# First layer of a graph network on one core: W0's lower half applied to x's rows in the preparation

## What is computed

```python
# first part: W is (512, 256)
support = segment_sum(edge_weight[:, None] * x[dst], src, N)
out = relu(concat([x, support], axis=1) @ W + b)
x = layernorm(x + out)
# second part: twice
#   xl = x @ Wl; xr = x @ Wr
#   attention of 8 heads over the edges and each node's own loop; x = x + gelu(tmp)
x = layernorm(x + second_part(x))
```

## Time and profile before

| | us |
|---|---|
| median of 3 runs | 2466.81 (2465.28 to 2472.84) |
| the profiled execution | 2466.77 |
| its span, first to last instruction | 2464.9 |
| busy in the span: TensorE / DVE / ACT / POOL | 1895.9 / 1766.4 / 1339.7 / 1449.3 |
| mean granted clock of TensorE | 0.916 of 2.4 GHz |

### The profile page before, as it was taken

The page is one execution under the profiler, slowest core; times in us unless marked ns, Lnnn a source line. Parts: engine busy times, 40 slices in busy tenths (PEclk is TensorE's granted clock), DMA queues, the critical chain, the costliest instruction groups (busy, mean ns, idle before and its releaser), DMA issues. The chain is left out here.

```text
span 2464.9 us, 38027 instructions
## 1 busy us (share of the span) xinstructions
PE 1895.9 (77%) x8650; PEld 1357.2 (55%) x8650; DVE 1766.4 (72%) x4022; ACT 1339.7 (54%) x5172; POOL 1449.3 (59%) x1606
## 2 busy tenths in 40 slices
PE   0655656556489998779999999986779999999975
PEld 0434434444267775456666666653456666666654
DVE  8544333333256666669999999988579999999976
ACT  0255555555300003438788777853458777787833
POOL 3277777787700001577777677735677777777712
PEclk9777788888789999989999999998899999999988
DMA  3287575665478871255555555541255555555542
GB/s 99 73 193 172 172 172 171 167 171 170 114 246 267 269 261 46 79 148 158 157 152 160 153 147 153 151 104 35 73 156 159 155 151 156 151 152 151 143 98 96
DMA packets 225173, 369.91 MB, mean 150 GB/s; under 512 B 40436, under 2 KB 168438, under 8 KB 224983
## 3 DMA queue, kind: packets, MB, share of 16 engines
q1 hardware_dynamic: 160311, 195.75, 28.6%
q0 software_dynamic: 64512, 171.82, 24.9%
q10 hardware_dynamic: 160, 0.20, 0.0%
HBM read 272.59 MB, written 101.50 MB: 152 GB/s over the span
## 5 line engine op out<-in xcount | busy, mean ns | idle before, releaser
L1150 POOL DMA_INDIRECT gath<-gather_table,SRCI x880 | 835.1, 949 | 323.4 <-issue 262.9
L1371 ACT ACTIVATE gath<-gath 128x32 f32<-128x32 f32 x3264 | 710.8, 306 | 0.0
L1202 PE MATMUL p_sums<-gath,OH 128*128 128x272 f32 x1760 | 474.4, 410 | 101.7 <-DVE gath L1097 60.8
L723 POOL DMA_INDIRECT rows_by_src<-gath,node x440 | 433.5, 985 | 137.5 <-issue 116.9
L657 PE MATMUL p_expd<-X,HOTS 128*128 x880 | 290.6, 490 | 230.2 <-DVE HOTS L616 218.6
L1202 PEld LDWEIGHTS p_sums<-gath,OH 128*128 128x128 f32 x1760 | 319.3, 194 | 215.7 <-issue 141.5
L657 PEld LDWEIGHTS p_expd<-X,HOTS 128*128 128x128 f32 x880 | 205.5, 244 | 304.7 <-issue 269.9
L1172 PE MATMUL p_expd<-node,LBC 128*128 x2640 | 327.5, 274 | 0.0
L1172 PEld LDWEIGHTS p_expd<-node,LBC 128*128 128x128 bf16 x2640 | 260.3, 99 | 59.4 <-issue 1.7
L1244 DVE TENSOR_REDUCE scores<-work 128x32 f32<-128x1056 f32 x220 | 274.6, 1248 | 5.7
L1166 PE MATMUL p_expd<-gath,ident 128*128 128x512 f32 x440 | 236.9, 620 | 39.7 <-DMA gath<-gather_table,SRCI 39.7
(11 more groups left out here) (291 smaller groups left out, 2749.3 us busy)
## 6 DMA issues: line engine op xcount, KB each, us to landing
gath<-rows_by_src SPq DMA_DIRECT2D x122, 514.0 KB
LBC<-hots_by_node SPq DMA_DIRECT2D x220, 128.0 KB
HOTS<-hots_by_edge SPq DMA_DIRECT2D x220, 128.0 KB, 2.4
LBC<-local_rows SPq DMA_DIRECT2D x110, 128.0 KB, 3.5
hots_by_node<-gath SPq DMA_DIRECT2D x110, 128.0 KB, 4.5
hots_by_edge<-gath SPq DMA_DIRECT2D x110, 128.0 KB, 3.1
gath<-gather_table,SRCI POOLq DMA_INDIRECT x880, 2.8
rows_by_src<-gath,node POOLq DMA_INDIRECT x440, 4.2
```

The lines of the kernel that those rows point to most:

```text
L723: pool.indirect_dma_start(sup_d[:, :], bass.IndirectOffsetOnAxis(POSI[:, i:i + 1], 0), U[:, q % 4, g, :], None, bounds_check=EP - 1, oob_i ...
L1150: pool.indirect_dma_start(ROWS[:, i % (RING * G), 0:XW], None, tab_d[:, :], bass.IndirectOffsetOnAxis(SRCI[:, i:i + 1], 0)).then_inc(gathe ...
L1202: ins = pe.matmul(sums[k][:, 0:RW], OH[:, a % 2, g, :], slots(a, g, g + 1)[:, 0, :], start=(g % 2 == 0), stop=(g % 2 == 1))
L1371: ins = act.activation(R[:, h * C:(h + 1) * C], R[:, h * C:(h + 1) * C], ACT.Copy, scale=R[:, D + h:D + h + 1])
```

## The change

- In the preparation, x is loaded from ACT's queue near the start, and W0's lower half into W0B. TensorE turns each tile of x and multiplies it by W0's lower half, 22 tiles ahead of the products at L472 and 3 behind the sum at L478; ACT copies both (`flat`, `kept`) into TURNED.
- The scatter stage takes rows of TURNED in place of x, and its sums with the upper half and the bias go into SUP.
- The sum stage adds on top of that; POOL's clearing goes.
- The linear stage has no transposes and products of "h". hidden() is one instruction a tile, with the statistics of a group together. The remainder moves from DVE to POOL.

```diff
-        FIRST_PART = gath[:, 4 * G * UW:4 * G * UW + NT * D].rearrange("p (t d) -> p t d", d=D)
+        TURNED = node[:, 9984:9984 + NT * D].rearrange("p (t d) -> p t d", d=D)
...
@@ preparation, SP's queue
-                    sp.dma_start(Xv[:, 0:NT - 1, :], x[0:(NT - 1) * P, :].rearrange("(t p) d -> p t d", p=P)).then_inc(x_loaded, 16)
-                    sp.dma_start(Xv[0:TAIL, NT - 1, :], x[(NT - 1) * P:N, :]).then_inc(x_loaded, 16)
...
@@ preparation, ACT
                     load_edges(act, SIi, src, src_in)
+                    act.dma_start(W0B.rearrange("p (k n) -> p k n", k=2), W0[2 * P:4 * P, :].rearrange("(k p) n -> p k n", p=P)).then_inc(w0_in, 16)
+                    act.wait_ge(pad_set, 4)
+                    act.dma_start(Xv[:, 0:NT - 1, :], x[0:(NT - 1) * P, :].rearrange("(t p) d -> p t d", p=P)).then_inc(x_loaded, 16)
+                    act.dma_start(Xv[0:TAIL, NT - 1, :], x[(NT - 1) * P:N, :]).then_inc(x_loaded, 16)
+
+                    def flat(t):
+                        act.wait_ge(x_turned, t + 1)
+                        if t >= 2:
+                            act.wait_ge(x_prod, t - 1)
+                        act.activation(XTP[:, t % 2, :], psum_tr[t % 2][:, 0:D], ACT.Copy).then_inc(x_flat, 1)
+
+                    flat(0)
+                    for t in range(NT):
+                        if t + 1 < NT:
+                            flat(t + 1)
+                        act.wait_ge(x_prod, t + 1)
+                        act.activation(TURNED[:, t, :], psum_tr[2 + t % 2][:, 0:D], ACT.Copy).then_inc(x_kept, 1)
...
@@ preparation, TensorE
+                    def by_weights(first, last):
+                        for t in range(first, last):
+                            if t + 1 < NT:
+                                turn(t + 1)
+                            pe.wait_ge(x_flat, t + 1)
+                            if t >= 2:
+                                pe.wait_ge(x_kept, t - 1)
+                            for k in range(2):
+                                ins = pe.matmul(psum_tr[2 + t % 2][:, 0:D], XTP[:, t % 2, k * P:(k + 1) * P], W0B[:, k * D:(k + 1) * D],
+                                                start=(k == 0), stop=(k == 1))
+                            ins.then_inc(x_prod, 1)
...
+                    pe.wait_ge(consts, 12)
+                    pe.wait_ge(x_loaded, 32)
+                    pe.wait_ge(w0_in, 16)
+                    turn(0)
+                    by_weights(0, PART_B)
                     pe.wait_ge(consts, 13)
                     pe.wait_ge(ranks_ready, 1)
...
                     ins.then_inc(pos_summed, 1)
+                    by_weights(PART_B, NT)
+                    pe.wait_ge(x_kept, NT)
                     pe.wait_ge(rows_ready, 1)
...
@@ scatter stage, DVE and TensorE
-                            dve.tensor_tensor(FIRST_PART[:, t, :], turn[t % 2][:, 0:D], VEC[:, 0, :], ALU.add).then_inc(x_added, 1)
+                            dve.tensor_tensor(SUP[:, t, :], turn[t % 2][:, 0:D], VEC[:, 0, :], ALU.add).then_inc(x_added, 1)
...
-                                            Xv[:, bass.ds(tiles[g // 2], 1), :], start=True, stop=True)
+                                            TURNED[:, bass.ds(tiles[g // 2], 1), :], start=True, stop=True)
...
@@ sum stage, POOL
-                    pool.memset(SUP, 0.0).then_inc(cleared, 1)
...
@@ linear stage, POOL
+                        remainder(pool, t, LR[:, t % DEEP, 1, 0:D], first_of, last_of, rest_of)
                         if t:
                             last_part(pool, t - 1, second_of, last_of)
                         if t in CLEAR:
-                            pool.wait_ge(turned_s, NT)
+                            pool.wait_ge(plus, NT)
...
@@ linear stage, TensorE
+                    transpose(0)
+                    for t in range(NT):
+                        if t + 1 < NT:
+                            transpose(t + 1)
+                        pe.wait_ge(flat_x, t + 1)
+                        if t >= 2:
+                            pe.wait_ge(lin_copied, t - 1)
...
@@ linear stage, DVE
-                        dve.wait_ge(prod_h, t + 1)
-                        dve.tensor_tensor(O[:, t % 2, :], psum_h[t % 2][:, 0:D], FIRST_PART[:, t, :], ALU.add).then_inc(plus, 1)
-                        dve.wait_ge(plus, t + 1)
-                        link(dve.scalar_tensor_tensor(Xv[:, t, :], O[:, t % 2, :], 0.0, Xv[:, t, :], ALU.max, ALU.add))
-                        ins = dve.bn_stats(STATS[:, t, 0:6], Xv[:, t, :])
+                        dve.scalar_tensor_tensor(Xv[:, t, :], SUP[:, t, :], 0.0, Xv[:, t, :], ALU.max, ALU.add).then_inc(plus, 1)
                         if t + 1 in BORDER:
+                            dve.wait_ge(plus, t + 1)
+                            for s in range(BORDER[BORDER.index(t + 1) - 1], t + 1):
+                                ins = dve.bn_stats(STATS[:, s, 0:6], Xv[:, s, :])
...
-                            remainder(dve, t - 1, LR[:, (t - 1) % DEEP, 1, 0:D], first_of, last_of, rest_of)
```

More of the change, by code:

```diff
@@ L226, in build @@
             PAST = JUNK[:, 0:G * NJ].rearrange("p (g j) -> p g j", g=G)
-            rows = [part[:, NT * EB + k * G * P:NT * EB + (k + 1) * G * P].rearrange("p (g q) -> p g q", g=G)[0:IR]
-                    for part in (gath, node) for k in range(6)]
+            low_rst = RST[:, :, :].rearrange("p w e -> p (w e)")
+            rows = [part[:, at + k * G * P:at + (k + 1) * G * P].rearrange("p (g q) -> p g q", g=G)[0:IR]
+                    for part, at in ((gath, NT * EB), (low_rst, G * P)) for k in range(6)]
+            W0B = WB[:, 0:2 * D]
+            XTP = HOTS[:, :, :].rearrange("p s n -> p (s n)")[:, 0:2 * D].rearrange("p (s d) -> p s d", s=2)
             PS, PD, PP, PW, PV2, PN, VAL, ST, RS, LC, EN = rows[:11]
@@ L810, in first_part, with remainder @@
             act.activation(PARTS3[:, t, 0, :], rows, ACT.Copy).then_inc(first_of, 1)
-        def remainder(dve, t, rows, first_of, last_of, rest_of):
-            dve.wait_ge(first_of, t + 1)
+        def remainder(eng, t, rows, first_of, last_of, rest_of):
+            eng.wait_ge(first_of, t + 1)
             if t >= 4:
-                dve.wait_ge(last_of, t - 3)
-            dve.tensor_tensor(REST[:, t % 4, :], rows, PARTS3[:, t, 0, :], ALU.subtract).then_inc(rest_of, 1)
+                eng.wait_ge(last_of, t - 3)
+            eng.tensor_tensor(REST[:, t % 4, :], rows, PARTS3[:, t, 0, :], ALU.subtract).then_inc(rest_of, 1)
         def second_part(act, t, rest_of, second_of):
@@ L892, in _, with evacuate @@
                 def _(act):
[L893 to L895 removed]
+                    def evacuate(t):
+                        act.wait_ge(turned_x, t + 1)
                         if t >= 2:
[L897 to L898 removed]
+                            act.wait_ge(prod_o, t - 1)
+                        act.activation(XTX[:, t % 2, :], psum_x[t % 2][:, 0:D], ACT.Copy).then_inc(flat_x, 1)
                     def rows(t):
@@ new lines, in transpose @@
+                    def transpose(t):
+                        if t in BORDER:
+                            pe.wait_ge(normed, BORDER.index(t) + 1)
+                        if t >= 2:
+                            pe.wait_ge(flat_x, t - 1)
+                        for k in range(2):
+                            ins = pe.transpose(psum_x[t % 2][:, k * P:(k + 1) * P], Xv[:, t, k * P:(k + 1) * P], ident[:, :])
+                        ins.then_inc(turned_x, 1)
+                    transpose(0)
+                    for t in range(NT):
+                        if t + 1 < NT:
+                            transpose(t + 1)
+                        pe.wait_ge(flat_x, t + 1)
+                        if t >= 2:
+                            pe.wait_ge(lin_copied, t - 1)
+                        for k in range(2):
+                            pe.matmul(psum_o[t % 2][:, :], XTX[:, t % 2, k * P:(k + 1) * P], WB[:, 2 * k * D:2 * (k + 1) * D],
+                                      start=(k == 0), stop=(k == 1))
+                        for k in range(2):
+                            ins = pe.matmul(psum_l[t % 2][:, 0:H], XTX[:, t % 2, k * P:(k + 1) * P], WA[:, k, :],
+                                            start=(k == 0), stop=(k == 1))
+                        ins.then_inc(prod_o, 1)
@@ L1009, in _ @@
                             normalize(roots[i])
-                        if kind == "o" and t >= 1:
-                            remainder(dve, t - 1, LR[:, (t - 1) % DEEP, 1, 0:D], first_of, last_of, rest_of)
                         if kind == "o" and t >= 2:
                             tile(t - 2)
-                    remainder(dve, NT - 1, LR[:, (NT - 1) % DEEP, 1, 0:D], first_of, last_of, rest_of)
                     tile(NT - 2)
```

71 lines of the change are left out of this document (13 added, 58 removed).

## The result

The changed kernel takes 2441.82 us (median of four runs, 2437.04 to 2444.1) where the kernel before takes 2468.35 (2465.28 to 2472.84): ratio 0.9895, interval 0.9878 to 0.9911. The profiled execution is one of the four, 2437.04 us with a span of 2435.2. Against the profiled execution of before that is 29.7 us less; the forecast was 31.6 less. The profiled execution is the fastest of the four: between the medians the gain is 26.5 us.

A forecast was written before the change was run, and what follows sets the result against it. Stages end at barriers, so their gains pass whole to the end; POOL was to pace the changed linear stage. 2466.8 + 2.4 (clock) + 0 (scatter) + 0 (sum) - 34.0 (linear) = 2435.2 us, range 2425 to 2448.

The forecast's parts named there:

- x's load: Preparation: x's two DMAs move from SP's queue to ACT's; ACT's queue held from about 4 to 14 us, cost 0.
- rival E: Preparation: x lands late and the 22 tiles run at the low clock, +16 us, total 2448.8; chance 0.04.
- The tiles by W0's half: Preparation: 22 tiles 1.09 us apart, 24 us from 20.2, fit before p_off at 58.34; three more after p_pos; cost 0.
- The clock term: Preparation: TensorE's clock falls in the idle time before p_off, slowing p_pos and three small products; +2.4 us, bounds 0 to +5.
- rival C: Preparation: the clock doesn't fall, so the total is the forecast less 2.4, 2432.8 us; chance 0.12.
- Scatter and sum: Scatter stage: same shapes and queues, 0 within ±2 us; sum stage: POOL's clearing goes, cost and gain 0.
- Linear, lead: Start of linear stage: first x transpose at 934.5 instead of 942.07, first ACT copy at 939.3, POOL's first instruction at 939.9.
- Linear, POOL's time a tile: Linear stage: POOL's three instructions, lengthened by DVE, set the pace at 2.42 us a tile, plus 6.0 for memsets; stage -34.0 us.
- rival A: Linear stage: TensorE is the bound at 2.34 us a tile, gain 40.0 us, total 2429.2; chance 0.17.
- Linear, DVE "hidden": Linear stage: DVE's 2.0 us a tile plus perhaps 0.6 of waits stays hidden, as it normalises four or five tiles ahead.
- The last words of the prediction: Linear stage: the forecast is wrong if DVE, not POOL, is what the others wait for.
- rival D: Linear stage: POOL so slow that the kernel gets slower, break-even 3.74 us a tile; at 4.0, total 2474.7; chance 0.03.

## Why the prediction was right, and where it wasn't

**x's load: right.** Cost 0. The load held ACT's queue 5.66 us, the tiles began at 20.04, and the run with the load on SP prices the opposite, rival E's late x, at 12 to 14 us.

**The tiles by W0's half: right.** After the first few they come 1.08 to 1.09 us apart, as in the earlier trace rows, and are through at 46.4. That holds for the chips of this speed. In the four traces from the slower chip TensorE stands 9.5 to 10.9 us in all between these products, mostly with no releaser that the trace shows. The tiles end at about 63 there, and p_off starts at 62.9 to 63.9, some 5 us late; the cause stays open.

**The clock term, +2.4: wrong; it was 0.** Failed step: "The granted clock was 1.00 in 74 to 80 us, so p_pos ran on the 2.4 GHz level though TensorE had idled 38 us before it." The size was right (2.1 by the 16.73 above), but the kernel before paid it too. I should have read the spacing of its passes beside the column. The fall after the new work did come, with a granted clock of 0.50 from 52 to 64 us in the trace after, and it changed nothing. So rival C has the number for this term and not the reason: it said that the clock would stay up.
The Trainium skill (TensorE: Matmul & The Clock Gate, Part 1: The HAM clock gate), which I had weighed and set aside, was right here: an idle engine starts on the lower level. The 0.65 us passes agree.

**Preparation, rest: +1.0 not forecast.** DVE's L445 waits for POOL's gather until 95.24. Six more traces with the same preparation put the scatter's first product 0.6 us earlier to 1.7 later than the kernel before had it (101.59), so this is no more than play.

**Scatter and sum: right.** Together with all behind them -0.8 us: scatter +1.3, sum -0.9, the later stages -1.2. The sum's first add comes at 691.40, 9.5 us after the stage's first load; before it was 9.7, with POOL's memset in it.

**Linear, lead: right.** From the stage's start to POOL's first instruction 10.9 us, forecast 11.4.

**Linear, POOL's time a tile: somewhat too high, and wrong in role.** From 940.75 to 1012.08 POOL has 71.3 us. Less 6.1 for the memsets and 5.13 idle in the large gap, 60.1 are left for 25 tiles, or 2.40 us a tile, which looks like the forecast's 2.42. But another 3.8 us of it are nine short waits for ACT; without them POOL needs 2.25 us a tile, less than TensorE's 2.34. The pace is TensorE's: 18 distances of 2.33 or 2.34. Only from 997.11 on, with two of its memsets still ahead, does POOL never wait, and there it ends the stage: the tail is 7.5 us, 4.4 without memsets. The profile fits rival A with a wait in it. Without the collisions of the two instructions 2431.6 was measured, near rival A's 2429.2, but in part by luck: rival A holds 2.4 us for the clock, which cost nothing, and 5.1 for a tail that took 6.6.

**Linear, DVE "hidden": wrong, and this is the 4 us.** Failed step: "DVE has five instructions of 0.34 a tile and small ones, 2.0 us, ... but it normalises four or five tiles ahead, and afterwards has only two instructions a tile: hidden." I had charged the collisions to POOL alone. DVE's own instructions grew as much: weighting 0.66 us in the mean for 0.50, normalisation 0.70 for 0.43. For 50 instructions that is (0.16 + 0.27) x 25 = 11 us more, the 1.9 of the memset included. The head start ended at the last span, the only one with five tiles, and a memset fell on it. TensorE stood 5.21 us, POOL behind it 5.13, and the clock added 1.9. The last words of the prediction named this as what would make it wrong. The runs confirm it from both sides: with the collisions of these two taken away the stage is 74.6, with DVE's queue merely reordered 84.5.
The Trainium skill (SBUF — State Buffer, Who interferes with whom) has a rule for this: a DVE instruction with at most one SBUF input, outside the two-port modes, doesn't contend with GpSimd. The trace agrees: 405 to 422 ns for all 25 weightings with the second operand in PSUM. The old normalisation, with one tile and two columns in SBUF, did collide; which mode it ran in no run shows. I had weighed that page's rule only for what it does to POOL.

**Result against the forecast.** Profiled, 2466.8 became 2437.0, forecast 2435.2: linear +4.1, clock -2.4, preparation's gather +1.0, rest -0.8. That the sum is off by 1.8 only is in part luck: two of the errors have opposite signs, and the profiled execution was the fastest of four. Between the medians the gain is 26.5 us (22.9 when the changed kernel ran again on another chip), 5 to 9 short of the 31.6 forecast.

One sum of rival D is off: (1041.6 - 1.2 - 939.9 - 6.0) / 25 is 3.78, not 3.74. Nothing else hangs on it.

## What to carry to other kernels

Where an instruction is moved from DVE to POOL, price the collision on both sides: the row of a lengthened POOL instruction has a lengthened DVE instruction beside it, and the one that TensorE waits for counts. Try an operand in PSUM before moving work: here it brought 12 us with two small edits, 9 to 11 of them in the linear stage. And when an engine that idled starts again, read the level of the clock from the spacing of its passes, not from a column that has shown nothing but 1.00 since the start.

## What I had not expected of the hardware

- DVE's normalisation has its operands in SBUF, one tile and two columns, and takes 0.41 us alone. Beside POOL's additions its median is 0.75, and one beside a memset took 2.30. The same with one operand in PSUM as an operation of two tensors takes 0.472 to 0.482, in every one of 50 cases.
- A wait of TensorE can cost more than its length. After 1.48 us the next four passes took 1.88 us, after 2.04 us 3.47, after 2.34 us 3.35, after 3.31 us 3.21 to 3.40 and after 5.21 us 3.39 to 3.62. It isn't a matter of length alone: with the remainder back on DVE they took 2.57 after 2.94 us, and the clock was still low in the tile behind.
- POOL's three additions a tile take 2.35 us (sum of the three means) beside the colliding DVE, and 2.18 when DVE reads from PSUM. DVE's two instructions take 1.36 and, free of it, 0.82 (0.41 each; 0.88 with the operands in PSUM). The collision is dearer for DVE than for POOL.
